# Gated cross-attention and a quantised feed-forward: PE's turns and value products in pairs, and a new order for the first two tiles

## The reference, cut to what matters

```
# x, ctx: (16, 64, 512); every one of the 16 batches is a 64 x 512 matrix
n_x, n_c = layernorm(x) then instance_norm, instance_norm(ctx)     # over the 512
qp = Wq @ n_x + bq ; kp = Wk @ n_c + bk ; sp = Ws @ ctx + bs
attn = softmax(qp.T @ kp)                    # 512 x 512 per batch
mean = attn applied to sp ; mean_sq = attn applied to sp * sp
std  = sqrt(relu(mean_sq - mean * mean))
x = x + tanh(g_xattn) * (n_c * std + mean)
w = (weight_q - 8) * scale + zero            # 512 x 512, in 4 groups of 128
x = x + tanh(g_ffn) * layernorm(x) @ w.T
```

## Time and profile before

| what | value |
|---|---|
| time, median of 3 runs | 185.67 us (185.67 to 186.62) |
| the profiled execution's own time | 186.42 us |
| its span, first to last instruction | 184.6 us |
| PE busy | 167.2 us (91%) |
| DVE busy | 141.0 us (76%) |
| POOL busy | 120.4 us (65%) |
| ACT busy | 118.0 us (64%) |

### The profile page before, as it was taken

How to read it: one execution, slowest core, us unless ns; L and a number is a source line. 1 busy time by engine, 2 the same in 40 slices (tenths; PEclk the granted TensorE clock), 3 DMA queues, 4 the chain that set the end, 5 groups by cost and what they waited for, 6 DMA issues and landing times.

```text
span 184.6 us, 3489 instructions
## 1 busy us (share of the span) xinstructions
PE 167.2 (91%) x1128; PEld 147.1 (80%) x1128; DVE 141.0 (76%) x311; ACT 118.0 (64%) x261; POOL 120.4 (65%) x145
## 2 busy tenths in 40 slices
PE   1554999999999999999999999999999979789992
PEld 0432889999999999999999999998789867567881
DVE  2897696689859887986988798676159679988851
ACT  2253575978598678859867885995569995232110
POOL 1455586917955896799589679944328959966310
PEclk9999999999999999999999999999999999999999
DMA  6408566883796699679679966356100000111212
GB/s 169 166 21 202 186 159 138 237 201 86 184 319 153 155 287 245 162 216 286 139 170 249 283 145 153 78 134 151 44 0 0 4 0 0 57 62 60 111 57 114
DMA packets 14321, 25.75 MB, mean 139 GB/s; under 512 B 2336, under 2 KB 2464, under 8 KB 14304
## 3 DMA queue, kind: packets, MB, share of 16 engines
q1 hardware_dynamic: 14304, 25.54, 52.2%
HBM read 9.67 MB, written 2.10 MB: 64 GB/s over the span
## 4 chain that ended last, share of the span: by engine, by line
PE 76%; DVE 9%; ACT 4%; issue 4%; POOL 3%; DMA 2%; SPq 0%; ACTq 0%; POOLq 0%
PE pv_bank L322 28%; PE turn_bank L306 14%; PE score_bank L296 8%; PE score_bank L297 8%; PE side_bank L333 3%; PE score_bank L377 3%; PE score_bank L371 3%; PE score_bank L370 3%; DVE X L667 2%; DMA CTX<-in_context 2%; PE side_bank L342 2%; ACT probs L442 1%; PE side_bank L283 1%; DVE result L692 1%; DVE stats L673 1%
## 5 line engine op out<-in xcount | busy, mean ns | idle before, releaser
L831 POOL TENSOR_SCALAR probs<-probs,rden 128x512 f32<-128x512 f32 x64 | 50.9, 796 | 32.2 <-DVE rden L623 32.0
L322 PE MATMUL pv_bank<-probs_t,values 128*128 128x128 f32 x512 | 67.7, 276 | 0.0
L442 ACT ACTIVATE probs<-score_bank,neg_max 128x512 f32<-128x512 f32 x64 | 44.1, 690 | 31.4 <-DVE neg_max L616 30.8
L322 PEld LDWEIGHTS pv_bank<-probs_t,values 128*128 128x128 f32 x512 | 62.4, 192 | 2.1 <-issue 1.7
L616 DVE TENSOR_REDUCE neg_max<-score_bank 128x1 f32<-128x512 f32 x64 | 43.5, 682 | 15.0 <-PE score_bank L297 14.4
L306 PE MATMUL turn_bank<-ident,probs 128*128 128x128 f32 x256 | 38.8, 275 | 1.1 <-ACT probs_t L450 1.0
L450 ACT COPY probs_t<-turn_bank 128x512 f32<-128x512 f32 x64 | 37.1, 581 | 3.2 <-PE turn_bank L306 3.0
L306 PEld LDWEIGHTS turn_bank<-ident,probs 128*128 128x128 f32 x256 | 31.1, 142 | 5.7 <-POOL probs L831 1.1
L296 PE MATMUL score_bank<-c_both,q_both 128*128 128x512 f32 x64 | 29.3, 458 | 2.3 <-ACT q_with_x L494 2.3
L297 PE MATMUL score_bank<-c_with_bias,q_with_x 128*128 128x512 f32 x64 | 26.4, 412 | 0.0
L296 PEld LDWEIGHTS score_bank<-c_both,q_both 128*128 128x128 f32 x64 | 13.0, 202 | 4.6 <-issue 2.9
(11 more groups left out here) (99 smaller groups left out, 243.6 us busy)
## 6 DMA issues: line engine op xcount, KB each, us to landing
c_both<-c_hi SPq DMA_DIRECT2D x30, 128.0 KB, 2.6
X<-in_x SPq DMA_DIRECT2D x8, 256.0 KB, 3.0
CTX<-in_context SPq DMA_DIRECT2D x8, 256.0 KB, 4.1
ctx_now<-in_context SPq DMA_DIRECT2D x8, 256.0 KB, 2.9
sz<-in_scales_zeros SPq DMA_DIRECT2D x4, 512.0 KB, 6.7
out<-result SPq DMA_DIRECT2D x8, 256.0 KB, 2.0
q_with_x<-x_hi SPq DMA_DIRECT2D x15, 128.0 KB, 2.3
c_with_bias<-c_lo SPq DMA_DIRECT2D x15, 128.0 KB, 2.9
```

Source lines behind the costliest of these rows:

```text
L322: last = pe.matmul(pv_bank[b][:, P * j:P * j + P], values[t % 2][:, i, b, :, :].rearrange("p a c -> p (a c)"), probs_t[g % PROBS_T][:, P * ...
L442: act.activation(probs[g % PROBS][:, :], score_bank[g % SBANKS][:, :], ACT.Exp, bias=neg_max[:, c:c + 1], accum_out=den[:, c:c + 1]).then_ ...
L831: pool.tensor_scalar(probs[g % PROBS][:, :], probs[g % PROBS][:, :], rden[:, c:c + 1], 1.0, ALU.mult, ALU.mult).then_inc(probs_done, 1)
```

## The change

PE takes two chunks at a time: both turns, then two weighs. probs_t gets a fourth buffer. On the other engines some helpers move to another position c: keep_mean(t-1, 1) on ACT from c = 2 to 3; on DVE variance(t-1, 1) from 3 to 5, with_mean(t-1) from 5 to 6, scale_weights from 6 to 7; on POOL relu(t-1) at c = 4 becomes relu(t-2) at c = 1 and, for tile 6, at the end of the last tile. average_weights goes in two groups of two.

The start is written anew. The parameters are loaded from ACT's queue. The matmul for A signals as soon as it is done, ahead of the two for the biases, which have another bank and a semaphore of their own. x_hi of tiles 0 and 1, c_hi of tile 1 and the biases are copied by ACT instead of DVE, c_both of tile 0 by POOL instead of ACT. DVE's first maxima stand between the statistics of tile 1 and not behind them. project(1) comes after turn(2) instead of before scores(3). SP waits for each part of the stacking by itself. A helper spin is there for extra matmuls while PE waits, but all its counts are zero.

```diff
-    SBANKS, PROBS, PROBS_T = 3, 4, 3
+    SBANKS, PROBS, PROBS_T = 3, 4, 4
+    SPIN = (0, 0, 0, 0, 0)
@@ sync
-            sp.dma_start(X[:, 0, :], x_tiles[0]).then_inc(first_loaded[0][0], DMA)
-            sp.dma_start(params_sb[:, :], params).then_inc(params_loaded, DMA)
-            sp.dma_start(CTX[:, 0, :], context_tiles[0]).then_inc(first_loaded[0][1], DMA)
+            load(0, *first_loaded[0])
             load(1, *first_loaded[1])
             load_ctx_now(0)
+            sp.wait_ge(c_hi_done, 1)
+            stack(0, 1, *x_and_c_hi_copies)
+            sp.wait_ge(q_hi_done, 1)
+            stack(0, 1, *q_hi_copies)
             sp.wait_ge(c_lo_done, 1)
-            stack(0, 1, *x_and_context_copies)
+            stack(0, 1, *c_lo_copies)
             sp.wait_ge(q_lo_done, 1)
-            stack(0, 1, *q_copies)
+            stack(0, 1, *q_lo_copies)
@@ tensor
             for g in range(AHEAD_S):
                 scores(g)
-            pe.wait_ge(q_lo_done, 1)
-            project(1)
+            value_product(0)
             scores(AHEAD_S)
-            value_product(0)
+            turn(0)
+            for g in range(1, LAST, 2):
+                t, c = divmod(g, CHUNKS)
+                if g + AHEAD_S < LAST:
+                    scores(g + AHEAD_S)
+                    scores(g + AHEAD_S + 1)
+                if c == 7 and t + 2 < TILES:
+                    pe.wait_ge(s_kept, t + 2)
+                    project(t + 2)
+                turn(g)
+                if g + 1 < LAST:
+                    turn(g + 1)
+                if g == 1:
+                    pe.wait_ge(q_lo_done, 1)
+                    project(1)
+                if c == 3 and t + 1 < TILES:
+                    value_product(t + 1)
+                if t == TILES - 2 and c >= 5:
+                    for group in ((0, 1), (2, 3))[(c - 5) // 2]:
+                        average_weights(group)
+                if g > 1:
+                    weigh(g - 2)
+                weigh(g - 1)
             turn_x(0)
-            weigh(LAST - 2)
             weigh(LAST - 1)
@@ scalar
+            act.dma_start(params_sb[:, :], params).then_inc(params_loaded, DMA)
             act.copy(w_turned[:, :], turn_bank[0][:, 0:2 * P]).then_inc(w_turned_kept, 1)
+            act.wait_ge(w_multiplied, 1)
+            act.copy(w_a_hi[:, :], pv_bank[1][:, 0:P]).then_inc(w_hi_ready, 1)
+            act.wait_ge(xn_done, 1)
+            act.copy(x_hi[0][:, :], xn[:, :]).then_inc(x_hi_done, 1)
...
             for g in range(AHEAD_E):
                 exponentials(g)
+            act.wait_ge(xn_done, 2)
+            act.copy(x_hi[1][:, :], xn[:, :]).then_inc(x_hi_done, 1)
@@ scalar, loop
+                    if g == 0:
+                        act.wait_ge(ctxn_done, 2)
+                        act.copy(c_hi[1][:, :], CTX[:, 1, :]).then_inc(c_hi_done, 1)
-                    if c == 0 and t + 1 < TILES:
+                    if c == (1 if t == 0 else 0) and t + 1 < TILES:
                         keep_q_hi(t + 1)
-                    if c == 2 and t > 0:
+                    if c == 3 and t > 0:
                         keep_mean(t - 1, 1)
@@ vector
-            first_statistics()
+            first_x_statistics()
+            ctx_statistics(0)
             normalise_x(0)
-            keep_x_hi(0)
+            finish_first_ctx_statistics()
...
-            keep_q_lo(0)
             x_statistics(1)
+            maximum(0)
+            keep_q_lo(0)
             ctx_statistics(1)
+            maximum(1)
+            reciprocal(0)
             finish_statistics(1)
+            maximum(2)
+            reciprocal(1)
             normalise_x(1)
-            keep_x_hi(1)
-            dve.wait_ge(gates_ready, 1)
-            for g in range(AHEAD_S):
-                maximum(g)
-                if g > 0:
-                    reciprocal(g - 1)
             normalise_ctx(1)
-            keep_c_hi(1)
@@ gpsimd
+            pool.wait_ge(ctxn_done, 1)
+            pool.tensor_copy(c_both[0][0:C, :], CTX[0:C, 0, :]).then_inc(c_both_ready, 1)
+            pool.wait_ge(c_both_ready, 1)
+            pool.tensor_copy(c_both[0][C:P, :], CTX[0:C, 0, :]).then_inc(c_both_ready, 1)
             split_c_lo(0)
+            normalise_probs(0)
             inverse_deviation(1)
+            normalise_probs(1)
+            split_x_lo(1)
```

More of the change, by code:

```diff
@@ L215, in stack @@
                                  src[t % 2][rows_of(b), :].bitcast(F32)).then_inc(stacked[b], DMA)
-            q_copies = [(q_both, 0, q_hi), (q_with_x, 0, q_hi), (q_both, 1, q_lo)]
-            x_and_context_copies = [(q_with_x, 1, x_hi), (c_both, 0, c_hi), (c_both, 1, c_hi), (c_with_bias, 0, c_lo)]
+            x_and_c_hi_copies = [(q_with_x, 1, x_hi), (c_both, 0, c_hi), (c_both, 1, c_hi)]
+            c_lo_copies = [(c_with_bias, 0, c_lo)]
+            q_hi_copies, q_lo_copies = [(q_both, 0, q_hi), (q_with_x, 0, q_hi)], [(q_both, 1, q_lo)]
+            all_copies = x_and_c_hi_copies + c_lo_copies + q_hi_copies + q_lo_copies
             def load_weights(g):
@@ L265, in _, with spin @@
         def _(pe):
+            def spin(n, b=0):
+                for _ in range(n):
+                    pe.matmul(pv_bank[b][:, 0:P], ident[:, :], ident[:, :], start=True, stop=True)
             def multiply_weights():
@@ L386, in _ @@
                 scores(g)
-            pe.wait_ge(q_lo_done, 1)
-            project(1)
+            value_product(0)
             scores(AHEAD_S)
-            value_product(0)
-            pe.wait_ge(ident_ready, 1)
-            for t in range(TILES):
-                for c in range(CHUNKS):
-                    g = CHUNKS * t + c
-                    if c % 2 == 1 and g + AHEAD_S < LAST:
-                        scores(g + AHEAD_S)
-                        scores(g + AHEAD_S + 1)
-                    if c == 7 and t + 2 < TILES:
-                        pe.wait_ge(s_kept, t + 2)
-                        project(t + 2)
-                    turn(g)
-                    if c == 3 and t + 1 < TILES:
-                        value_product(t + 1)
-                    if t == TILES - 2 and c >= 5:
-                        for group in ((0, 1), (2,), (3,))[c - 5]:
-                            average_weights(group)
-                    if g >= BEHIND_V:
-                        weigh(g - BEHIND_V)
+            spin(SPIN[4], 1)
+            turn(0)
[21 more added lines that the diff above has]
+                weigh(g - 1)
             turn_x(0)
-            weigh(LAST - 2)
             weigh(LAST - 1)
@@ L748, in _ @@
                         finish_statistics(t + 2)
-                    if c == 3:
-                        if t > 0:
-                            variance(t - 1, 1)
-                        if t + 2 < TILES:
-                            normalise_x(t + 2)
+                    if c == 3 and t + 2 < TILES:
+                        normalise_x(t + 2)
                     if c == 4:
@@ L760, in _ @@
                         if t > 0:
-                            with_mean(t - 1)
+                            variance(t - 1, 1)
                         if t + 2 < TILES:
@@ L915, in _ @@
                         weights_lo((2, 3, 5, 6).index(c))
+                    if t == TILES - 1 and c == 7:
+                        relu(TILES - 2)
                     if g + AHEAD_E < LAST:
```

83 lines of the change are left out of this document (44 added, 39 removed).

## The result

The kernel got slower: 192.65 us median (192.24 to 193.32) against 185.69 for the kernel before on the same chip, ratio 1.037 (1.032 to 1.041). The profiled execution took 192.24 with a span of 190.4, 5.8 us more than before. The forecast was 187.1, slower by 1.4, in a range that ended at 188.4: the sign was right, and the size was outside the range. Three executions, each over 1.5% longer than the fastest of its kernel, are left out of all ratios here: one of the kernel before (288 us), one of E11 (430) and one of E2 (190.53).

What follows compares the result with a forecast made beforehand. PE's own work was taken to bound the kernel from 25.71 us to the last scores. Start -0.8, pairs +1.85 and tail +0.35 summed to +1.4 us, giving 187.1 against 185.67, range 184.6 to 188.4.

Steps and rivals of the forecast that it cites:

- The bound: From 25.71 us to the last scores PE's own work sets the end; a change of order there can only lose.
- saving 0 from the same kind of work side by side: On PE, pairing turns and weighs saves 0, since switching between transposes and value matmuls shows no cost.
- the start to scores(8): New start: scores(0) at 11.7, scores(6) at 24.0, scores(8) at 29.4 instead of 30.19; -0.8 us, bounds -1.8 to +0.8.
- the tail: Tile 7: exponentials(63) later on ACT, turn_x(0) behind one more weigh; +0.35 us, between -0.3 and +1.0.
- the waits at c = 3: PE's second turn waits for ACT's copy: 0.42 us counted in each of tiles 2 to 5, 0.17 in tile 1.
- Rival 2: ACT's copies come in time, so the 1.85 us falls away and the sum is -0.5, faster; chance 0.18.
- Turns in pairs: The part on PE's new order and moved helpers in the middle; sum +1.85 us, bounds 0 to 2.3.
- With little to spare: At c = 1, ACT's copy was said to be just in time for the second turn, so no wait.
- The other rule: Start loads: if queues alternate, x lands near 4.1 instead of 3.8, gain 0.2 instead of 0.5, whole sum +1.7.
- Rival 3: PE's higher clock comes as late as before or later, start loses 0.2 to 0.8: 188.1 to 188.7; chance 0.1.
- Late normalised probabilities: At c = 3 they were ready about 0.1 us before the new turn; lateness raises the pairs' bound to 2.3.
- SP's finer waits: On SP, waiting for each stacking part separately costs nothing while the stacking lands ahead of PE.

Runs made afterwards that it cites:

- E11: The changed kernel with normalise_ctx(t+2) ahead of variance(t-1, 1) at c = 5 on DVE: 188.43 us, ratio 1.010 to the kernel before.
- E2: The changed kernel with PE's old order of turn and weigh (turn, weigh, turn, weigh): 188.72 us, ratio 1.011 to the kernel before.
- E1: The kernel before with only PE's loop in pairs and the fourth probs_t buffer: 189.58 us, ratio 1.016 to the kernel before.
- E3: The changed kernel with keep_mean, variance, with_mean, scale_weights and relu back at their old positions: 190.06 us, ratio 1.020 to the kernel before.
- E6: The changed kernel with variance, with_mean and keep_mean back at c = 3, 5 and 2: 190.23 us, ratio 1.021 to the kernel before.
- E7: The changed kernel with POOL's square_values behind normalise_probs at c = 6: 191.38 us, ratio 1.029 to the kernel before.
- E9: The kernel before with the new start and extra unread matmuls while PE waits (SPIN 10, 2, 4, 7, 0): 186.79 us, ratio 1.003.

## Why the prediction was wrong

**Right, in mechanism and size.** The bound (PE's own work between 25 us and the last scores); saving 0 from the same kind of work side by side; the start to scores(8), -0.78 for -0.8, with every point of its chain named above within 0.2 us; the tail, +0.43 for +0.35, of which only the sum was looked at; and the waits at c = 3, released by ACT's copy: 0.42 us a tile, as worked out. Tile 1 has the full 0.42 instead of 0.17, which makes 2.1 instead of 1.85. Rival 2 (the copies come in time) is refuted by E1 and E3. That the start fits to 0.02 us is in part luck: other profiles with this start reach scores(8) at 29.3 to 30.9, and E1, with the start of before, at 29.59.

**The step that failed.** It is in "Turns in pairs": "moving variance(t-1, 1) and the mean helps only what stands behind", "One small gain: c = 5 has variance in the place of with_mean, 0.06 us shorter", and "At c = 1, 5 and 7 no value product stood between the turns, and by the same reckoning the copy is there in time, at c = 1 with little to spare". The moved helpers were priced by their own durations, and what stands behind them was taken to be as long as before. But with_mean and variance differ in what POOL does beside them, and so in what the next instruction on DVE meets. From the start of normalise_ctx to that of maximum(8t+9) it was 0.84 us and is 1.35; with 0.15 ahead of it, this is the 0.66 by which the maximum comes later. ACT's exponential, the reciprocal and POOL's normalise_probs, square and c_lo stand behind it. "With little to spare" then became some 0.5 us more of wait a tile at c = 1, for the normalised probabilities and not for the copy, and 0.2 at c = 7, 4.1 us in all, of which the late load of tile 1 is 0.33. E6, E7 and E11 each take the collision away by another edit, and each time normalise_ctx is 0.92, 0.55 and 0.53 us and the waits it caused go.

The trace of before had it: normalise_ctx took 0.92 us there (the line at 80.50 above) and normalise_x, the same operation on the same shape, 0.54. A 0.4 us difference between two like instructions was an unread sign that something else ran beside one of them.

**The Trainium skill** (SBUF — State Buffer, "Who interferes with whom") says that VectorE and GpSimd share one pair of ports, that it is held for a whole instruction, and that the other then waits; it names VectorE instructions in a two-port mode or with two SBUF inputs. The traces agree in direction: 0.53 alone, 1.32 behind a square of 1.04 that began at the same time. It also fits that the variance, with one input in PSUM, held nothing back. A full wait and then a full 0.53 would have ended at 84.47; it ended at 84.22. By this rule the forecast should have asked of each moved DVE instruction what POOL does beside it.

The other rule was weighed in the forecast: **the Trainium skill** (DMA: Bandwidth & Descriptors, "Queues, rings and completion order") lets SP's and ACT's queues take turns. x landed at 3.90, 0.37 later than before and 0.28 ahead of the parameters: in the direction of the rule, nearer to the value that the sum had taken.

**The range.** Its upper end was built from bounds of terms that I had listed (the copy 0 to 2.3, the start, the tail, the clock). The helpers had been given no bound at all: they were written off in a sentence. Late normalised probabilities were allowed for, but at c = 3 alone. Rival 3 did not decide this profile, where the clock held. The small loss behind the start, the late load of the fourth tile, was missed too: "SP's finer waits cost nothing while the stacking lands ahead of PE" left out the loads queued behind the stacking.

## What to carry to other kernels

When an edit moves an elementwise instruction on VectorE, price it together with what GpSimd runs at that time, before and after; compare the durations of like instructions in the trace first, for one that is much longer than its twin shows where the two engines meet. Put the instruction that collides at the moment at which the other engine still waits for its data: the swap of two lines gave 4.2 us here in one kernel and 0.7 in the other. And a gain in the start is only a gain if the loads for the later tiles move forward with it.

## What the runs showed of the hardware

- VectorE's normalise_ctx, 128x512, f32, takes 0.53 us alone or when it starts first (E11), 0.92 beside the end of a GpSimd instruction and 1.32 when a GpSimd multiplication of 1.04 starts with it, or 1.44 when it starts 0.12 earlier beside the instruction before that (E2); it then ends about 0.28 us after the other. The multiplication took 1.04 beside it and 1.03 without (E7), and 1.20 where it started within it (before). scale_weights took 0.68, 1.10, 1.45, 1.53 or 1.67 by its place and its neighbours on POOL.
- PE, after it had risen to the higher level, fell back at about 20 to 22 us, after pauses that began at 17, in four of eleven profiles with the new start (granted clock 0.55 to 0.61 in the stretches read, against 1.00); extra matmuls that ended before the pauses did not prevent it.
- The first group of extra matmuls (twenty records) took 4.64 us (E9) and held the first useful one up by 1.7, so work put in front of it is not free.
